# Expert stage: gate logits on four column tiles, and the second expert bias added on VectorE

## Chip, cores and metric

One core of one Trainium2 chip runs the whole program. The metric is the device time of one execution in microseconds; less is better. The number to compare with is the median of the runs.

## What is computed

Two layers on x of shape (4, 256, 256). The first is a cross attention with small heads. The second is a transformer block: layer norm, attention with 16 heads of 128, and a mixture of four experts on the 1024 tokens. The change touches only the experts:

```python
def _moe(h, w_gate, we1, be1, we2, be2):          # E = 4, I = 256, TOP_K = 2
    x = h.reshape(-1, d)                          # 1024 tokens x 256
    raw = softmax(x @ w_gate)                     # gate logits: 1024 x 4
    top_vals, top_idx = top_k(raw, TOP_K)
    w = softmax(top_vals)
    comb = zeros((t, E)).at[rows, top_idx].add(w) # gates: two per token are not 0
    hmid = gelu(einsum('td,edi->tei', x, we1) + be1)
    eout = einsum('tei,eid->ted', hmid, we2) + be2
    return einsum('te,ted->td', comb, eout)
```

`be2` is the second bias, one row of 256 per expert; it enters the output as gate times bias, summed over the experts. The block's result is multiplied by tanh of a scalar and added to x.

## The kernel before

The work is written out by hand, engine by engine, with semaphores between the engines; each engine runs its list in order. There is no scheduler. The tokens are eight tiles of 128 (`NT = 8`), in pairs of two tiles per batch entry (`B = 4`).

The experts come last. All four experts are computed for every token, and the gates weigh the results. TensorE splits each number into a high and a low part and makes three matmuls of each product (`three`, L1192). Its steps:

- `second_turn(b)`: four transposes that turn the normed rows of pair b; VectorE writes them, scaled, as `h2T` (L785, counted by `c_hT`), ScalarE makes the high part `hH`, GpSimd the low part `hL` (L446).
- `middle(n)`: n runs over 16; half the tokens (c = n // 8) by one half of an expert's inner columns, 6 matmuls of 512 columns into bank n % 2. It waits until ScalarE has read that bank (`c_gelu`, n - 1).
- ScalarE: `gelu` of the bank (L611) into `G`, and the high part into `GH` (L616); GpSimd subtracts for the low part `GL` (L450, counted by `c_gL`).
- `expert_out(m)`: m runs over 8 (half of the tokens times expert), 24 matmuls of 256 columns. It waits for `c_gL` 2m + 2, and from m = 2 on for VectorE's accumulation of m - 2 (`c_acc`).
- VectorE: for each m four instructions L1036 that add gate times result to `yacc`, and for the last expert of a half L1043, which finishes the output rows (`c_fin`) so that SyncE may store them.

The gates run beside this. TensorE makes the logits behind `expert_out(0)`: `h2T` is stationary (128 columns), the gate weights move (4 columns), eight tiles by two halves of the sum, in fp32, which is two instructions for one matmul (L1351). VectorE copies them (L981) and works out the gates in some 30 small instructions, with two exponentials on ScalarE between (L604, L606). ScalarE takes these in its own list ahead of `gelu(4)`; each change between exponential and gelu has a load of its function table. Then TensorE turns the gates (L1358, behind `middle(5)`), VectorE copies them to `V` as `combT` (L1017, L1018), TensorE multiplies them by `be2_sb`, four rows of stationary and moving data (L1366, behind `middle(6)`), and VectorE adds the four banks to `yacc` (L1023), before the first L1036.

TensorE's list there is: `second_turn(2)`, `middle(2)`, `second_turn(3)`, `middle(3)`, `expert_out(0)`, logits, `expert_out(1)`, `middle(4)`, `middle(5)`, turned gates, `middle(6)`, bias matmuls, `middle(7)`, `expert_out(2)`, and then `middle(8)`, `middle(9)`, `expert_out(3)` and so on, with `expert_out(6)` and `expert_out(7)` at the end with nothing between.

The cross attention at the start of the program has a step that uses four column tiles already, `x_values` (L1145): the stationary block has 32 columns, and four matmuls write partitions 0, 32, 64 and 96 of one bank.

```python
ins = pe.matmul(bank[4][32 * n:32 * (n + 1), t * P:(t + 1) * P], v_slots[:, XG * (2 * b + kt) + k // 3, :],
                probs[:, p % 4, n * P:(n + 1) * P], start=(z != 2), stop=(z != 1))
```

`stg` holds incoming attention weights; its last use is by GpSimd and ScalarE in the attention stage (`wqk_ready`, `wv_ready`). SyncE's list has 16 loads at the start, then 64 swaps, each as two DMAs of half a tile (L266 to L268), then the four stores of the output.

## Time and profile before

| | us |
|---|---|
| median of 3 runs | 505.7 |
| all runs | 510.95, 505.7, 505.22 |
| the profiled execution, device time | 508.26 |
| its span, first to last instruction | 506.4 |
| TensorE busy (3396 instructions) | 453.2 |
| VectorE busy (1163) | 367.1 |
| ScalarE busy (613) | 239.6 |
| GpSimd busy (318) | 232.8 |

The mean granted clock of TensorE over the span is 0.975 of full. The profile gives instructions by their line in the kernel; PE is TensorE's matmul, PEld its weight load, DVE VectorE, ACT ScalarE, POOL GpSimd, SP SyncE. A matmul's duration includes the time that it takes to run through the array, so the starts of successive ones say more than the durations. In the profile's rows the tile names have no digits, so `be2_sb` reads `be_sb` there.

### The profile page before, as it was taken

The numbers are of one execution on the slowest core, as the hardware profiler recorded it, in microseconds if no ns is written. First come the engines' busy times: TensorE is split into PE (matmuls) and PEld (weight loads), VectorE is DVE, ScalarE is ACT, GpSimd is POOL, SyncE is SP. The second block draws the span as 40 slices with busy tenths as digits, with TensorE's granted clock in tenths as the row PEclk, the third lists the DMA queues.
The fourth block names the chain that finished last, engine by engine and source line by source line (L and its number), as shares of the span: only waits on it lengthen the run. The fifth ranks groups of instructions, "written<-read, shape, count | busy, mean of one in ns | idle before, by whom it ended". The sixth has DMA issues, their size and how long they took to land.

```text
span 506.4 us, 10710 instructions
## 1 busy us (share of the span) xinstructions
PE 453.2 (89%) x3396; PEld 386.2 (76%) x3396; DVE 367.1 (72%) x1163; ACT 239.6 (47%) x613; POOL 232.8 (46%) x318
## 2 busy tenths in 40 slices
PE   0289998898777999999999999999999998689996
PEld 0166666675565899999999999999999997578895
DVE  5876669776557878788788887887877878835544
ACT  2026555453113555555655546556455565164342
POOL 5945709710345545446446445346454431162342
PEclk9999999999979999999999999999999998897899
DMA  8100000200123343352342532532533310000011
GB/s 286 28 3 1 2 1 3 84 1 1 23 62 84 72 119 84 84 145 64 78 133 58 143 85 62 145 74 52 144 83 83 77 29 0 2 0 2 0 43 42
DMA packets 19881, 31.41 MB, mean 62 GB/s; under 512 B 6020, under 2 KB 8200, under 8 KB 19848
## 3 DMA queue, kind: packets, MB, share of 16 engines
q1 hardware_dynamic: 15928, 22.31, 18.1%
q10 hardware_dynamic: 3920, 8.69, 5.7%
q8 instruction: 18, 0.29, 0.2%
q14 instruction: 15, 0.12, 0.1%
HBM read 13.16 MB, written 1.05 MB: 28 GB/s over the span
## 4 chain that ended last, share of the span: by engine, by line
PE 80%; DVE 12%; POOL 3%; issue 3%; DMA 1%; ACT 1%; ACTq 0%; DVEq 0%
PE bank L1192 42%; PE bank L1272 5%; PE bank L1235 5%; PE bank L1263 4%; PE bank L1145 3%; PE bank L1112 3%; PE bank L1273 3%; PE bank L1234 3%; PE bank L1126 2%; PE bank L1130 2%; PE bank L1090 1%; PE bank L1113 1%; PE bank L1128 1%; PE bank L1069 1%; DMA rows_sb<-in_rows 1%
## 5 line engine op out<-in xcount | busy, mean ns | idle before, releaser
L401 POOL TENSOR_TENSOR room<-room,qk_room 128x512 f32<-128x512 f32 x64 | 82.3, 1287 | 102.8 <-DMA qk_room<-qk_room 102.6
L542 ACT ACTIVATE probs<-sm,nm 128x128 f32<-128x128 f32 (+1 forms) x128 | 57.3, 448 | 116.2 <-DVE nm L917 116.2
L1192 PE MATMUL bank<-hH,qk_parts 128*128 128x512 f32 x256 | 81.0, 398 | 0.0
L840 DVE SCALAR_TENSOR_TENSOR qk_room<-bank,qk_bias,cst_sb 128x512 f32<-128x512 f32 x64 | 48.0, 750 | 37.2 <-PE bank L1192 35.8
L1192 PE MATMUL bank<-hL,qk_parts 128*128 128x512 f32 x128 | 62.4, 488 | 6.6 <-DVE room L840 5.7
L1192 PEld LDWEIGHTS bank<-hH,qk_parts 128*128 128x128 f32 x256 | 48.8, 191 | 10.1
L840 DVE SCALAR_TENSOR_TENSOR room<-bank,qk_bias,cst_sb 128x512 f32<-128x512 f32 x64 | 47.6, 743 | 0.0
L1192 PE MATMUL bank<-woH,o_parts 128*128 128x256 f32 x256 | 47.2, 283 | 0.0
L810 DVE TENSOR_REDUCE nxm<-bank 128x2 bf16<-128x512 f32 (+1 forms) x48 | 32.5, 688 | 14.9 <-PE bank L1113 14.3
L500 ACT ACTIVATE probs<-bank 128x512 f32<-128x512 f32 x48 | 28.6, 596 | 26.1 <-PE bank L1130 25.4
L1192 PE MATMUL bank<-woL,o_parts 128*128 128x256 f32 x128 | 39.0, 305 | 1.1 <-DVE o_parts L905 1.1
L1192 PEld LDWEIGHTS bank<-woH,o_parts 128*128 128x128 f32 x256 | 40.0, 192 | 0.0
L1272 PE MATMUL bank<-probs,V 128*128 128x256 f32 x128 | 39.0, 387 | 0.6 <-DVE o_parts L905 0.6
L1192 PE MATMUL bank<-wvL,hH 128*128 128x256 f32 x128 | 39.3, 307 | 0.0
L1235 PE MATMUL bank<-room 128*128 128x256 f32 x128 | 38.2, 380 | 0.0
L1192 PE MATMUL bank<-wvH,hH 128*128 128x256 f32 x128 | 36.4, 284 | 0.0
L450 POOL TENSOR_TENSOR qk_parts<-G,o_parts 128x512 fp32r<-128x512 f32 x16 | 20.7, 1298 | 34.0 <-ACT o_parts L616 33.5
L1192 PE MATMUL bank<-wvH,hL 128*128 128x256 f32 x128 | 36.3, 283 | 0.0
L1263 PE MATMUL bank<-cst_sb,probs 128*128 128x128 f32 x192 | 31.7, 274 | 4.9 <-DVE probs L961 4.9
L351 POOL TENSOR_TENSOR qk_parts<-stg,qk_parts 128x256 fp32r<-128x256 f32 x32 | 23.8, 743 | 26.5 <-ACT qk_parts L566 26.5
L556 ACT ACTIVATE o_parts<-bank,bv_pair 128x256 fp32r<-128x256 f32 x64 | 30.3, 474 | 11.6 <-PE bank L1273 10.8
L1263 PEld LDWEIGHTS bank<-cst_sb,probs 128*128 128x128 f32 x192 | 24.4, 140 | 14.6 <-DVE probs L961 6.8
(200 smaller groups left out, 1242.2 us busy)
## 6 DMA issues: line engine op xcount, KB each, us to landing
qk_room<-qk_room SPq DMA_DIRECT2D x128, 128.0 KB, 2.3
stg<-in_wqkv ACTq DMA_DIRECT2D x6, 768.0 KB, 4.6
stge<-in_we ACTq DMA_DIRECT2D x7, 256.0 KB, 3.2
stg<-in_wqkv SPq DMA_DIRECT2D x2, 768.0 KB, 6.4
stgo<-in_wo ACTq DMA_DIRECT2D x6, 256.0 KB, 3.6
x_sb<-in_x SPq DMA_DIRECT2D x4, 256.0 KB, 6.2
out_y<-yacc SPq DMA_DIRECT2D x4, 256.0 KB, 2.3
cst_sb<-in_cst SPq DMA_DIRECT2D x1, 520.0 KB, 6.9
```

Source lines behind the costliest of these rows:

```text
L351: pool.tensor_tensor(wqkL[:, c], stg[:, k, :, r * HD:(r + 1) * HD], wqkH[:, c].bitcast(F32), ALU.subtract).then_inc(s["wqk_ready"], 1)
L401: pool.tensor_tensor(v, v, qk_sw[:, q, :], ALU.subtract).then_inc(s["rope_done"], 1)
L450: pool.tensor_tensor(GL[:, (n // 2) % 2, n % 2, :], G[:, n % 2, :], GH[:, (n // 2) % 2, n % 2, :].bitcast(F32), ALU.subtract).then_inc(s[" ...
L500: act.activation(probs[:, p % 4, :], PT_B[p % 2][:, :], ACT.Exp).then_inc(s["s_exp"], 1)
L542: ins = act.activation(PR[:, q, a:e], sm[:, q, a:e], ACT.Exp, bias=nm[:, q, t:t + 1], scale=-1.0, accum_out=rs[:, q, t:t + 1])
L556: act.activation(oH[:, ((j - 2) // 2) % 2, q, :], bank[3][:, 0:256], ACT.Identity, bias=head_bias(j)).then_inc(s["b_oH"], 1)
L810: dve.tensor_reduce(nxm[:, m % 3, a:a + len(heads)], S_B[p % 2][:, :].rearrange("p (h n) -> p h n", h=len(heads)), AX.X, ALU.max, negate=T ...
L840: return dve.scalar_tensor_tensor(out.rearrange("p (b t) -> p b t", b=2), O_B[q][:, :].rearrange("p (b t) -> p b t", b=2), qk_bias[:, c:c ...
L1192: ins = pe.matmul(outp, l, r, start=(m == 0), stop=(m == n - 1))
L1235: pe.matmul(S_B[j % 2][:, P:3 * P], QT[:, 2 * r, second], QT[:, 2 * r + 1, both], start=True, stop=True).then_inc(s["b_s"], 1)
L1263: ins = pe.transpose(bank[2][:, n * P:(n + 1) * P], PR[:, 1 - q, n * P:(n + 1) * P], ident)
L1272: pe.matmul(bank[3][:, 0:256], V[:, 2 * b, r * HD:(r + 1) * HD], PTs[:, q, 0:256], start=True, stop=False)
```

## The change

The logits are made the other way round and earlier. The gate weights are stationary, padded with zeros from 4 to 32 columns (GpSimd clears `w_gate_sb` as its first instruction, and SyncE's load of it waits for that). For each half of the sum, four matmuls of 256 moving columns of `h2T`, one for each pair of tiles, write partitions 32b to 32b + 31 of bank 5. They stand in front of `expert_out(0)`. VectorE copies the 128x256 result to `nh`, TensorE turns it with two transposes in front of `expert_out(1)`, and VectorE copies four of each 32 columns as the logits. The gates are worked out as before.

The gates are no longer turned, and the bias is no longer a matmul. SyncE loads `be2`, repeated on all 128 partitions, into the space of `stg`, after the last swap. For each m VectorE adds gate times bias row to its four tiles of `yacc` (four new instructions, all operands in SBUF), before it waits for TensorE's result of that m.

```diff
-        w_gate_sb = sb("w_gate_sb", [P, KT, E])
-        be2_sb = sb("be2_sb", [E, D])
+        w_gate_sb = sb("w_gate_sb", [P, KT, 32])
...
+        be2_rows = stg[:, 0:2, :, :].rearrange("p w k n -> p (w k n)").rearrange("p (e n) -> p e n", e=E)
...
# SyncE
-            sp.dma_start(w_gate_sb[:, :, :], w_gate).then_inc(s["d_small"], 16)
-            sp.dma_start(be2_sb[:, :], be2).then_inc(s["d_small"], 16)
+            sp.wait_ge(s["gate_zero"], 1)
+            sp.dma_start(w_gate_sb[:, :, 0:E], w_gate).then_inc(s["d_small"], 16)
...
             steps(sp, step)
+            sp.wait_ge(s["wqk_ready"], 4 * NP)
+            sp.wait_ge(s["wv_ready"], NP)
+            sp.dma_start(be2_rows, be2.rearrange("(o e) n -> o e n", o=1).to_broadcast([P, E, D])).then_inc(s["d_be"], 16)
...
# GpSimd
+            pool.memset(w_gate_sb[:, :, :], 0.0).then_inc(s["gate_zero"], 1)
             link(pool.memset(room[:, 0:NT * XG * VP], 0.0))
...
# VectorE
             dve.wait_ge(s["c_logit"], 1)
-            link(dve.tensor_copy(Gt(0, 32), bank[5][:, 0:32]))
+            dve.tensor_copy(nh[:, 0, :], bank[5][:, 0:256]).then_inc(s["c_lgT"], 1)
+            dve.wait_ge(s["c_lg_pe"], 1)
+            link(dve.tensor_copy(Gt(0, 32).rearrange("p (b t e) -> p t b e", t=2, e=E),
+                                 bank[4][:, 0:256].rearrange("p (t b w) -> p t b w", t=2, b=B)[:, :, :, 0:E]))
...
-            dve.tensor_tensor(Gt(0, 32), Gt(120, 32), Gt(152, 32), ALU.add).then_inc(s["c_comb"], 1)
-            dve.wait_ge(s["c_combT_pe"], 1)
-            dve.tensor_copy(combT[:, 0:4, :].rearrange("p t n -> p (t n)"), bank[4][0:E, :])
-            dve.tensor_copy(combT[:, 4:8, :].rearrange("p t n -> p (t n)"), bank[5][0:E, :]).then_inc(s["c_combT"], 1)
-            for b in range(B):
-
-                dve.wait_ge(s["c_be"], b + 1)
-                y = yacc[:, 2 * b:2 * b + 2, :].rearrange("p t n -> p (t n)")
-                dve.tensor_tensor(y, y, bank[4 + b % 2][:, :], ALU.add).then_inc(s["c_init"], 1)
-            dve.wait_ge(s["c_init"], B)
+            link(dve.tensor_tensor(Gt(0, 32), Gt(120, 32), Gt(152, 32), ALU.add))
+            dve.wait_ge(s["d_be"], 16)
+            dve.wait_ge(s["b_yadd"], NU // 2)
 
             for m in range(2 * E):
 
                 c, e = divmod(m, E)
                 for hf in range(2):
                     b = 2 * c + hf
-                    dve.wait_ge(s["c_exp_pe"], 2 * m + hf + 1)
                     if m:
                         dve.wait_ge(s["c_acc"], 2 * (m - 1) + hf + 1)
+                    for t in range(2):
+                        n = 2 * b + t
+                        ins = dve.scalar_tensor_tensor(yacc[:, n, :], be2_rows[:, e, :], gate[:, 4 * n + e:4 * n + e + 1], yacc[:, n, :],
+                                                       ALU.mult, ALU.add)
+                    ins.then_inc(s["c_be"], 1)
+                for hf in range(2):
+                    b = 2 * c + hf
+                    dve.wait_ge(s["c_exp_pe"], 2 * m + hf + 1)
+                    dve.wait_ge(s["c_be"], 2 * m + hf + 1)
...
# TensorE
             middle(3)
+            pe.wait_ge(s["c_hT"], B)
+            pe.wait_ge(s["d_small"], 16)
+            pe.wait_ge(s["b_yadd"], NU // 2)
+            for k in range(KT):
+                for b in range(B):
+                    ins = pe.matmul(bank[5][32 * b:32 * (b + 1), 0:256], w_gate_sb[:, k, :], h2T[:, k, 256 * b:256 * (b + 1)],
+                                    start=(k == 0), stop=(k == 1))
+            ins.then_inc(s["c_logit"], 1)
             expert_out(0)
-            pe.wait_ge(s["c_hT"], B)
-            pe.wait_ge(s["d_small"], 32)
-            for n in range(NT):
-                for k in range(KT):
-                    ins = pe.matmul(bank[5][:, E * n:E * (n + 1)], h2T[:, k, n * P:(n + 1) * P], w_gate_sb[:, k, :], start=(k == 0), stop=(k == 1))
-            ins.then_inc(s["c_logit"], 1)
+            pe.wait_ge(s["c_lgT"], 1)
+            for t in range(2):
+                ins = pe.transpose(bank[4][:, t * P:(t + 1) * P], nh[:, 0, t * P:(t + 1) * P], ident)
+            ins.then_inc(s["c_lg_pe"], 1)
             expert_out(1)
             middle(4)
             middle(5)
-            pe.wait_ge(s["c_comb"], 1)
-            for n in range(NT):
-                ins = pe.transpose(bank[4 + n // 4][0:E, (n % 4) * P:(n % 4 + 1) * P], gate[:, E * n:E * (n + 1)], ident)
-            ins.then_inc(s["c_combT_pe"], 1)
             middle(6)
-            pe.wait_ge(s["c_combT"], 1)
-            for b in range(B):
-                if b >= 2:
-                    pe.wait_ge(s["c_init"], b - 1)
-                for t in range(2):
-                    ins = pe.matmul(bank[4 + b % 2][:, 256 * t:256 * (t + 1)], combT[:, 2 * b + t, :], be2_sb[:, :], start=True, stop=True)
-                ins.then_inc(s["c_be"], 1)
```

TensorE's list between the end of `middle(3)` and the first matmul of `expert_out(0)`, in the kernel before; a row names line, operation, output and inputs, and the semaphores waited for:

```order
L1192 MATMUL bank<-hL,weH 128x512
L1192 MATMUL bank<-hH,weL 128x512
L1192 MATMUL bank<-hH,weH 128x512
L1192 MATMUL bank<-weL,o_parts 128x256 [waits b_yadd,c_gL]
L1192 MATMUL bank<-weH,qk_parts 128x256
L1192 MATMUL bank<-weH,o_parts 128x256
```

The same place in the changed kernel, where the helper of the matmuls is at L1199 and the logits at L1358:

```order
L1199 MATMUL bank<-hL,weH 128x512
L1199 MATMUL bank<-hH,weL 128x512
L1199 MATMUL bank<-hH,weH 128x512
L1358 MATMUL bank<-qk_room,w_gate_sb 32x256 [waits b_yadd,d_small,c_hT]
L1358 MATMUL bank<-qk_room,w_gate_sb 32x256 x7
L1199 MATMUL bank<-weL,o_parts 128x256 [waits b_yadd,c_gL]
```

Eight logit matmuls have moved in front of `expert_out(0)`; before, sixteen of 128x4 stood behind it.

VectorE's list from the last instruction of the gates to the first accumulation, before:

```order
L1015 TENSOR_TENSOR gate<-gate 128x32 [waits dve_seq]
L1017 COPY V<-bank 4x512 [waits c_combT_pe]
L1018 COPY V<-bank 4x512
L1023 TENSOR_TENSOR yacc<-yacc,bank 128x512 [waits c_be] x4
L1036 SCALAR_TENSOR_TENSOR yacc<-bank,gate,yacc 128x256 [waits c_exp_pe,c_init]
L1036 SCALAR_TENSOR_TENSOR yacc<-bank,gate,yacc 128x256
```

And in the changed kernel, with the bias at L1034 and the accumulation at L1043:

```order
L1021 TENSOR_TENSOR gate<-gate 128x32 [waits dve_seq]
L1034 SCALAR_TENSOR_TENSOR yacc<-stg,gate,yacc 128x256 [waits b_yadd,d_be,dve_seq]
L1034 SCALAR_TENSOR_TENSOR yacc<-stg,gate,yacc 128x256 x3
L1043 SCALAR_TENSOR_TENSOR yacc<-bank,gate,yacc 128x256 [waits c_be,c_exp_pe]
L1043 SCALAR_TENSOR_TENSOR yacc<-bank,gate,yacc 128x256
```

The wait for turned gates and the four additions of banks are gone, and four bias instructions stand in front of the four accumulations, here and for each later m.

## Rows read from the trace of the kernel before

**Rows 1.** Stretches of the expert stage: busy time and count per engine, granted clock, DMA.
```profile
454.40:456.20 1.80, 1.80 (x11) 1.80 (x10) 0.00 (x0) 0.00 (x0) 0.00 (x0) 0.50 0.00 0
456.20:461.05 4.85, 4.85 (x24) 4.85 (x25) 3.94 (x24) 0.23 (x1) 0.00 (x0) 0.50 0.02 3
...
471.30:474.70 3.40, 3.40 (x15) 2.90 (x15) 3.09 (x8) 1.32 (x2) 0.78 (x1) 0.50 0.00 0
```

**Rows 2.** Timeline of TensorE: start, duration, line, tiles, shape, count.
```profile
448.95 0.28 PE L1192 MATMUL bank<-weL,o_parts 128*128 128x256 f32 x1
...
451.78 4.56 PE L1351 MATMUL bank<-w_gate_sb,qk_room 128*128 128x4 f32 x32
456.20 0.56 PE L1192 MATMUL bank<-weL,o_parts 128*128 128x256 f32 x1
...
461.30 0.40 PE L1192 MATMUL bank<-hL,weH 128*128 128x512 f32 x1
```

**Rows 3.** Timeline of TensorE, further on, to the start of `middle(8)`.
```profile
464.10 1.04 PE L1358 MATMUL bank<-cst_sb,gate 128*4 128x128 f32 x8
...
466.50 3.90 PE L1366 MATMUL bank<-be_sb,V 4*128 4x256 f32 x16
470.33 0.50 PE L1192 MATMUL bank<-hL,weH 128*128 128x512 f32 x1
...
476.24 0.40 PE L1192 MATMUL bank<-hL,weH 128*128 128x512 f32 x1
```

**Rows 4.** Timeline of TensorE in the cross attention: four column tiles.
```profile
61.77 0.43 PE L1145 MATMUL bank<-probs,room 128*32 128x128 f32 x8
62.13 0.28 PE L1112 MATMUL bank<-yacc,qk_room 128*128 128x256 bf16 x1
```

**Rows 5.** Timeline of VectorE; in brackets the idle time before and its releaser.
```profile
456.38 0.19 DVE L981 COPY gate<-bank 128x32 f32<-128x32 f32 x1 [7.63 <-PE bank L1351]
...
462.28 0.19 DVE L1015 TENSOR_TENSOR gate<-gate 128x32 f32<-128x32 f32 x1
...
471.16 3.23 DVE L1036 SCALAR_TENSOR_TENSOR yacc<-bank,gate,yacc 128x256 f32<-128x256 f32 x8
```

**Rows 6.** Timeline of ScalarE around `gelu(4)`.
```profile
461.29 1.28 ACT L611 ACT_TABLE_LOAD   x1
462.90 0.69 ACT L611 ACTIVATE G<-bank,cols_sb 128x512 f32<-128x512 f32 x1 [0.33 <-PE bank L1192]
```

**Rows 7.** Timeline of GpSimd: the low halves, early and late.
```profile
464.33 2.67 POOL L450 TENSOR_TENSOR qk_parts<-G,o_parts 128x512 fp32r<-128x512 f32 x2 [11.16 <-ACT o_parts L616]
...
496.13 2.69 POOL L450 TENSOR_TENSOR qk_parts<-G,o_parts 128x512 fp32r<-128x512 f32 x2 [2.93 <-ACT o_parts L616]
```

**Rows 8.** Timeline of VectorE at the end: last pair of m = 6, first of m = 7.
```profile
498.93 0.88 DVE L1036 SCALAR_TENSOR_TENSOR yacc<-bank,gate,yacc 128x256 f32<-128x256 f32 x2 [0.53 <-PE bank L1192]
500.61 0.88 DVE L1036 SCALAR_TENSOR_TENSOR yacc<-bank,gate,yacc 128x256 f32<-128x256 f32 x2 [0.81 <-PE bank L1192]
```

**Rows 9.** Timeline of TensorE: two waits before the expert stage.
```profile
426.67 0.69 PE L1263 MATMUL bank<-cst_sb,probs 128*128 128x128 f32 x3 [1.53 <-DVE probs L961]
...
445.20 0.66 PE L1296 MATMUL bank<-cst_sb,nh 128*128 128x128 f32 x4 [1.78 <-DVE nh L892]
```

**Rows 10.** Stretches of one us behind those waits.
```profile
427.00:428.00 1.00, 1.00 (x5) 0.78 (x3) 0.93 (x6) 0.49 (x1) 0.00 (x0) 0.50 0.00 0
...
445.00:446.00 1.00, 0.80 (x6) 0.75 (x7) 0.89 (x4) 1.00 (x2) 0.48 (x1) 1.00 0.00 0
```

**Rows 11.** DMA issues: KB each, median us from issue to landing.
```profile
stg<-in_wqkv ACTq DMA_DIRECT2D x6, 768.0 KB, 4.6
```

**Rows 12.** VectorE beside GpSimd: timeline, and L1043's durations in ns, min/median/max.
```profile
434.74 1.26 POOL L446 TENSOR_TENSOR hL<-qk_room,hH 128x512 fp32r<-128x512 f32 x1 [9.27 <-ACT hH L593]
435.08 0.94 DVE L643 SCALAR_TENSOR_TENSOR small<-small 128x2 f32<-128x2 f32 x1
...
L1043 DVE SCALAR_TENSOR_TENSOR yacc<-yacc,small,x_sb x4: 752/752/937, 481.6 to 503.1; 128x512 f32<-128x512 f32 x4
```

More of the change, by code:

```diff
@@ L118, in build_kernel @@
         gate = sb("gate", [P, 512])
-        combT = V[0:E, 0:4, :].rearrange("p t n -> p (t n)").rearrange("p (t n) -> p t n", t=NT)
+        be2_rows = stg[:, 0:2, :, :].rearrange("p w k n -> p (w k n)").rearrange("p (e n) -> p e n", e=E)
         qn = sb("qn", [P, 2, D])
@@ L164, in build_kernel @@
         b_s b_max b_exp b_norm b_pt b_ptcopy b_pv b_oH b_oL b_wo b_yadd v_pe v_ready
-        c_nh c_tr c_hT c_hH c_h c_logit c_comb c_combT_pe c_combT c_be c_init c_mid c_gelu c_gH c_gL c_exp_pe c_acc c_fin"""
+        c_nh c_tr c_hT c_hH c_h gate_zero d_be c_logit c_lgT c_lg_pe c_be c_mid c_gelu c_gH c_gL c_exp_pe c_acc c_fin"""
         s = {n: sem(n) for n in names.split()}
```

## The prediction

> **What bounds the kernel now.** The page comes first: it shows TensorE as the busiest engine, most of the chain that ended last on it, and its granted clock below full in a few slices near the end. All that the change touches on the compute engines lies from 448.95 us on, so the next view is a table of stretches from there. TensorE is busy without a break in all eight up to 500 us, and in three of them, 454.4 to 461.05 and 471.3 to 474.7, the granted clock is 0.50 [rows 1], that is 1.2 of 2.4 GHz. The timeline of TensorE says what stood there. The gate logits (L1351, 32 instructions of 4 columns) hold it from 451.78 to 456.20, 4.42 us, and `expert_out(1)` behind them takes 461.30 - 456.20 = 5.10 us [rows 2], while `expert_out(0)`, the same 24 matmuls, takes 451.78 - 448.95 = 2.83. The turned gates (L1358) and the bias matmuls (L1366, 466.50 to 470.33) are followed by `middle(7)` and `expert_out(2)` in 476.24 - 470.33 = 5.91 us [rows 3]; at full clock these are 1.40 (half of 464.10 - 461.30) and 2.83. So this part is TensorE bound, and thin matmuls cost twice there: their own time, and the fallen clock behind them. The clock fell while TensorE was busy; what went before it was L1351, and the second time L1366.
>
> **What is removed.** L1351 4.42. Slow `expert_out(1)` 5.10 - 2.83 = 2.27. L1358 with the small gap ahead of L1366: 466.50 - 464.10 less `middle(6)`'s 1.40, 1.00. L1366 3.83. Slow clock behind it 5.91 - 4.23 = 1.68. Together 13.2 us of the chain.
>
> **What TensorE gets.** Eight logit matmuls of 32 stationary and 256 moving columns, in fp32 two instructions each, so 16. The nearest row has the same layout with 128 columns: eight instructions on four column tiles take 62.13 - 61.77 = 0.36 us [rows 4]. Twice the instructions and twice the columns give 1.44 at most if the tiles go on running side by side. One after another, 16 fp32 instructions of 256 columns are L1366's: 3.83 us [rows 3]. If four do run at once the lower end is a quarter, 0.96. I take 1.15, between the near ends, and keep 3.8 for a rival. The wait for the last `h2T` costs nothing: VectorE was done with it at 456.38 - 7.63 = 448.75 [rows 5]. Two transposes: four took 0.66 us to their last result [rows 9]; for two I take 0.5 until VectorE starts (ends 0.35 and 0.66), and 0.2 of TensorE's issue. VectorE's new copy to `nh`, 256 columns out of PSUM like one instruction of L1036 (0.40, rows 5), lies beside `expert_out(0)`'s 2.83.
>
> **Where the gate chain then ends.** The logits end at 448.95 + 1.15 = 450.1, `expert_out(0)` at 452.93, and VectorE starts on the gates at 453.43 where it was 456.38 [rows 5]: 2.95 us earlier. From there the chain runs unchanged on VectorE and ScalarE, so the table load behind the second exponential moves from 461.29 to 458.34 and ends at 459.62 [rows 6]; `gelu(4)` starts at 459.65. TensorE gets there earlier: transposes until 453.15, `expert_out(1)` until 455.98, `middle(4)` and `middle(5)` until 458.78. `middle(6)` needs the bank that `gelu(4)` reads in 0.69 us [rows 6], so it starts at 460.4: **a new wait of 1.6 us**. `middle(6)` and `middle(7)` end at 463.2. `expert_out(2)` needs GpSimd's low halves of `gelu(4)` and `gelu(5)`; that pair ended at 464.33 + 2.67 = 467.00, 4.10 after `gelu(4)`'s start at 462.90 [rows 6, 7], so now at 463.75: a second wait of 0.6 us. `expert_out(2)` ends at 463.8 + 2.83 = 466.65, where it was 476.24 [rows 3]: 9.6 us. The other way round, 13.2 less 1.15, 0.2, 1.6 and 0.6 gives 9.65. VectorE is ready in time: gates done at 462.28 + 0.19 - 2.95 = 459.5, then four bias and four accumulate instructions at 3.23/8 = 0.40 us each [rows 5], until 462.8, before 463.75.
>
> **The bias on VectorE.** It adds 32 instructions of 128x256, four per expert call. L1043, all in SBUF, takes 0.75 for twice the columns [rows 12], and L1036 0.40 with one operand in PSUM [rows 5]; I use 0.40, so 12.8 us in all (ends 0.35 and, held by GpSimd, the last rival's). Per call VectorE then has 8 x 0.40 = 3.2 us against TensorE's 5.6 (two `middle` and one `expert_out`), and the bias stands ahead of the wait for TensorE's result, in time where VectorE idles. The exception is the last call, for `expert_out(7)` follows `expert_out(6)` with no `middle` between. VectorE's last accumulate pair of call 6 starts at 498.93; four bias instructions follow, and six at 0.393 end at 501.29, where call 7 started at 500.61 [rows 8]. What is behind it is VectorE's own, so **0.7 us comes back at the end**.
>
> **The clock behind the new wait.** A wait of 1.53 us before 426.67 was followed by clock 0.50, one of 1.78 before 445.20 by 1.00 [rows 9, 10]. The new one of 1.6 is between them. If the clock falls there, it covers `middle(6)` to `expert_out(2)`; 3.4 us at half clock, as from 471.3, cost up to 1.7, of which some 0.6 hides in the wait for GpSimd: 1.1. Ends 0 and 1.7; as one row of two says so, I take half of 1.1, 0.5. In the Trainium skill, "TensorE: Matmul & The Clock Gate" (Part 1, "What's actually happening") has the slow level return from idleness, after a wholly idle period; by that the term would be 0 and the time 496.8. The trace disagrees twice, with a fall at 454.4 while TensorE was busy [rows 1, 2] and one after 1.53 us of idling; the measurement decides.
>
> **What costs nothing.** GpSimd's clearing of the gate weights stands at the start, ahead of its wait for the DMA of `rows_sb`, and is hidden by it. SyncE's wait for it comes before SyncE's twelfth DMA, when the clearing is long done. The 512 KB copy of the bias rows is issued after the last swap, near 410 us, and is needed at 459.5; 768 KB landed in 4.6 us [rows 11]. Without that cover it would cost about 3 us. The four additions L1023 and both copies to `V` leave VectorE beside TensorE's work and are not counted again.
>
> **Sum.** 9.6 - 0.7 - 0.5 = 8.4 us. The profiled execution took 508.26 us (span 506.4), so it would be 499.9; the median of the runs is 505.7, 2.6 below it, and I take the same 8.4 from it: **497.3 us**, 1.7% faster. About 2% (10.1 us) is what a measurement of this kernel can tell from no change, so this counts as the same.
>
> **Rivals.**
> *More than 10 us.* The clock stays up (0.5), the logits take 0.96 (0.2), and the unprofiled runs had one slow stretch more in this part (1.7), since its fall need not be the same in each run: 10.8, 494.9 us. For it: two stretches hang on thin matmuls; against: the median is 2.6 us shorter than the profiled execution, which may as well mean fewer slow stretches.
> *Tiles one after another.* 3.8 instead of 1.15, and the whole gate chain moves with it: 2.65, 500.0 us. Against it speaks the 0.36 of rows 4: eight of half the columns in turn would be near 0.96.
> *The slow clock is not won.* The wait at `middle(6)` grows or repeats and the clock falls as often as before: the gain lacks the 2.27 + 1.68 but the term of 0.5 goes with it, 4.9 us, 500.8. For it: 1.6 and 0.6 us waits close together. Against: behind 463.8 TensorE has no cause to wait.
> *Slower: VectorE held by GpSimd.* The bias instructions read two tensors from SBUF. A 128x2 instruction of this kind took 0.94 us beside a GpSimd subtraction of 1.26, and one L1043 of four 0.94 instead of 0.75 [rows 12]. Held by h each, VectorE needs 3.14 + 4h per call against 5.62: it is the bound from h = 0.62, all the gain is gone at 0.92, and at a whole GpSimd instruction (1.29) seven calls lose 18.8 us, 516.1. Against it: GpSimd works 2.69 of 5.62 us, and the bias falls in its gap (call 6 from 494.2 to 495.8; GpSimd ends at 493.2 and starts at 496.13) [rows 7]; one held instruction at 462.8 has 2.8 us of slack. "GPSIMD Engine Reference" (Specifications) in the Trainium skill names the same conflict, for VectorE instructions with two SBUF inputs, and the trace agrees with 0.94; it gives no price.
>
> **How the numbers follow.** Forecast 0.63, with a range of its own of 495.8 to 499.2 (the ends of logits, transposes and clock); over 10 us 0.13; tiles in turn 0.12; slow clock not won 0.09; VectorE held 0.03. The range holds the forecast's own, the two rivals near 500 and most of the fast one: 494.6 to 500.8. Faster by over 2% 0.17 (its rival and the forecast's edge), slower by over 2% 0.02, within 0.81.
>
> **What would show it.** Logits near 1.15 us behind `middle(3)`; gates on VectorE 2.9 us earlier; one wait of TensorE for ScalarE of about 1.6 us at `middle(6)` and one for GpSimd of about 0.6 at `expert_out(2)`; bias instructions of 0.4 to 0.5 us with none near 1; the last accumulates 0.7 late behind four of them; clock 1.00 from 449 to 460. I am wrong if the clock falls in the logits or right behind them, if the wait at `middle(6)` is over 2.5 us, or if VectorE is what TensorE waits for at any `expert_out`.

## The result, and the profile after

The changed kernel takes 500.04 us (median of 6 runs, 498.48 to 502.3) against 506.39 of the kernel before on the same chip (6 runs, 503.2 to 510.95). The ratio is 0.9878, with a 95% interval of 0.9849 to 0.9908: 6.35 us or 1.2% faster, less than the 2% that tells a kernel from no change. The forecast was 497.3, and the result lies within its range of 494.6 to 500.8, near the slow end. The gain itself was forecast at 8.4 us, and that lies outside the measured interval, which is 4.7 to 7.6 us: near three quarters of it came.

The profiled execution took 499.90 us (span 498.1), 8.4 less than the profiled one of before, which is exactly the predicted difference. That agreement is partly luck, as the experiments show, for the medians are 6.35 apart. Single executions scatter by 2 to 3 us either way, and much of it arises before the experts: `middle(3)` ended between 444.8 and 450.8 us in the fourteen traces of this study; why is not followed here. So below a **local stretch** is compared: from the start of the first TensorE instruction behind `middle(3)` to the end of the last VectorE instruction. It was 503.85 - 448.95 = 54.90 us before; the times ahead of it are left out.

First the page of the changed kernel: busy time by engine, and the chain that ended last, by engine and by line.

```profile
PE 441.2 (89%) x3342; PEld 375.2 (75%) x3358; DVE 382.8 (77%) x1190; ACT 239.6 (48%) x613; POOL 233.5 (47%) x319
...
PE 68%; DVE 24%; issue 4%; POOL 1%; DMA 1%; ACT 1%; SPq 0%; DVEq 0%; POOLq 0%
PE bank L1199 35%; PE bank L1279 5%; PE bank L1242 5%; PE bank L1270 4%; DVE yacc L1034 3%; PE bank L1241 3%; PE bank L1280 3%; PE bank L1152 2%; DVE yacc L1043 2%; PE bank L1119 2%; DVE nxm L813 2%; PE bank L1137 2%; PE bank L1097 1%; PE bank L1135 1%; DVE small L646 1%
```

TensorE lost 12 us of busy time and VectorE gained 16. New are the two yacc lines, 5% of the span: the chain that ended last runs through VectorE's bias (L1034) and accumulation (L1043), some 25 us of the end. That is the first sign of a new bound.

TensorE's timeline from `middle(3)`'s end to `middle(8)`'s start, which answers to [rows 2, 3]:

```profile
448.44 1.07 PE L1358 MATMUL bank<-qk_room,w_gate_sb 128*32 128x256 f32 x16
449.44 0.39 PE L1199 MATMUL bank<-weL,o_parts 128*128 128x256 f32 x1
...
452.37 0.38 PE L1364 MATMUL bank<-cst_sb,nh 128*128 128x128 f32 x2
452.51 0.37 PE L1199 MATMUL bank<-weL,o_parts 128*128 128x256 f32 x1
...
455.42 0.40 PE L1199 MATMUL bank<-hL,weH 128*128 128x512 f32 x1
...
459.73 0.50 PE L1199 MATMUL bank<-hL,weH 128*128 128x512 f32 x1 [1.35 <-ACT G L614]
...
463.04 0.39 PE L1199 MATMUL bank<-weL,o_parts 128*128 128x256 f32 x1 [0.25 <-POOL qk_parts L453]
...
465.98 0.40 PE L1199 MATMUL bank<-hL,weH 128*128 128x512 f32 x1
```

The logits take 449.44 - 448.44 = 1.00 us; `expert_out(1)` 455.42 - 452.51 = 2.91, where it was 5.10; and the two forecast waits are there. The bracket at 459.73 counts 1.35 us of idling, since the view lets a matmul last until it has run through the array. By starts it is 1.5: `middle(5)`'s last matmul started at 457.99 and one takes 0.23 of pace. From `middle(3)`'s end to `middle(8)` it is 465.98 - 448.44 = 17.54 us, against 27.29 before.

Stretches of time there, with the columns of [rows 1]: the granted clock, third from the end, is 1.00 in all.

```profile
450.00:454.00 4.00, 4.00 (x36) 4.00 (x35) 0.81 (x5) 1.94 (x3) 2.69 (x3) 1.00 0.00 0
454.00:458.00 4.00, 4.00 (x26) 3.49 (x24) 3.38 (x22) 0.52 (x2) 0.00 (x0) 1.00 0.00 0
458.00:462.00 4.00, 2.65 (x12) 1.87 (x11) 3.86 (x13) 3.67 (x6) 1.58 (x2) 1.00 0.01 4
462.00:466.00 4.00, 3.75 (x29) 3.26 (x28) 4.00 (x5) 2.38 (x4) 3.72 (x3) 1.00 0.01 2
```

The gate chain on VectorE, ScalarE and GpSimd, which answers to [rows 5 to 7]:

```profile
452.79 0.19 DVE L986 COPY gate<-bank 128x32 f32<-128x32 f32 x1 [2.79 <-PE bank L1364]
...
458.68 0.19 DVE L1021 TENSOR_TENSOR gate<-gate 128x32 f32<-128x32 f32 x1
```

```profile
450.44 1.28 ACT L607 ACT_TABLE_LOAD   x1
...
457.69 1.28 ACT L614 ACT_TABLE_LOAD   x1
458.99 0.69 ACT L614 ACTIVATE G<-bank,cols_sb 128x512 f32<-128x512 f32 x1
```

```profile
460.42 2.57 POOL L453 TENSOR_TENSOR qk_parts<-G,o_parts 128x512 fp32r<-128x512 f32 x2 [7.73 <-ACT o_parts L619]
463.27 2.99 POOL L453 TENSOR_TENSOR qk_parts<-G,o_parts 128x512 fp32r<-128x512 f32 x2 [0.28 <-ACT o_parts L619]
```

`middle(3)` ended 0.51 us earlier than in the trace of before. With that taken off, each link is within 0.25 us of where it was put: the gates begin at 452.79 (forecast 453.43), the table load ends at 458.97 (459.62), the pair of low halves at 462.99 (463.75).

VectorE from there to the end of the program. In the text, call m is `expert_out(m)` with what VectorE does for it, m from 0 to 7. L1034 is the bias, L1043 the accumulation, L1050 the last step of the rows of the output.

```profile
462.06 4.48 DVE L1034 SCALAR_TENSOR_TENSOR yacc<-stg,gate,yacc 128x256 f32<-128x256 f32 x4
466.46 1.65 DVE L1043 SCALAR_TENSOR_TENSOR yacc<-bank,gate,yacc 128x256 f32<-128x256 f32 x4
468.03 2.71 DVE L1034 SCALAR_TENSOR_TENSOR yacc<-stg,gate,yacc 128x256 f32<-128x256 f32 x4
...
474.71 1.76 DVE L1050 SCALAR_TENSOR_TENSOR yacc<-yacc,small,x_sb 128x512 f32<-128x512 f32 x1
...
485.55 3.74 DVE L1034 SCALAR_TENSOR_TENSOR yacc<-stg,gate,yacc 128x256 f32<-128x256 f32 x4
...
490.79 1.66 DVE L1034 SCALAR_TENSOR_TENSOR yacc<-stg,gate,yacc 128x256 f32<-128x256 f32 x4
492.37 0.86 DVE L1043 SCALAR_TENSOR_TENSOR yacc<-bank,gate,yacc 128x256 f32<-128x256 f32 x2
493.26 0.75 DVE L1050 SCALAR_TENSOR_TENSOR yacc<-yacc,small,x_sb 128x512 f32<-128x512 f32 x1
493.93 0.87 DVE L1043 SCALAR_TENSOR_TENSOR yacc<-bank,gate,yacc 128x256 f32<-128x256 f32 x2
494.84 0.75 DVE L1050 SCALAR_TENSOR_TENSOR yacc<-yacc,small,x_sb 128x512 f32<-128x512 f32 x1
```

And the two lines over the whole program, durations in ns (min/median/max):

```profile
L1034 DVE SCALAR_TENSOR_TENSOR yacc<-stg,gate,yacc x32: 470/475/1524, 458.9 to 492.0; 128x256 f32<-128x256 f32 x32
...
L1043 DVE SCALAR_TENSOR_TENSOR yacc<-bank,gate,yacc x32: 468/472/481, 460.5 to 494.3; 128x256 f32<-128x256 f32 x32
```

No row after 458.9 has a bracket: VectorE works without a break to the end. The same shape of instruction never takes over 481 ns in this trace with one operand in PSUM, and up to 1524 with all in SBUF; four of the latter take 1.66 us undisturbed and 4.48, 2.71, 2.80 or 3.74 when GpSimd subtracts beside them. The last of the four of call 1, and the GpSimd instruction beside it:

```profile
465.03 1.51 DVE L1034 SCALAR_TENSOR_TENSOR yacc<-stg,gate,yacc 128x256 f32<-128x256 f32 x1
464.78 1.48 POOL L453 TENSOR_TENSOR qk_parts<-G,o_parts 128x512 fp32r<-128x512 f32 x1
```

VectorE's ends at 466.54 and GpSimd's at 466.26. An instruction that takes so much longer beside GpSimd's than alone is called held below.

TensorE's last matmul ends at 491.77 and VectorE at 495.59, 3.82 us later. That **tail** was 503.85 - 501.98 = 1.87 before. The forecast allowed 0.7 more; it is 1.95.

### The profile page after: what moved, and what is told of

Its sections match the earlier page's. It is cut to its first block, busy times and chain, and to the rows that moved or that the text cites. A ratio compares the mean times of both kernels' runs of the same rounds, so it can differ in the third digit from the quotient of the medians.

```text
span 498.1 us, 10649 instructions
## 1 busy us (share of the span) xinstructions
PE 441.2 (89%) x3342; PEld 375.2 (75%) x3358; DVE 382.8 (77%) x1190; ACT 239.6 (48%) x613; POOL 233.5 (47%) x319
## 3 DMA queue, kind: packets, MB, share of 16 engines
HBM read 13.68 MB, written 1.05 MB: 30 GB/s over the span
## 4 chain that ended last, share of the span: by engine, by line
PE 68%; DVE 24%; issue 4%; POOL 1%; DMA 1%; ACT 1%; SPq 0%; DVEq 0%; POOLq 0%
PE bank L1199 35%; PE bank L1279 5%; PE bank L1242 5%; PE bank L1270 4%; DVE yacc L1034 3%; PE bank L1241 3%; PE bank L1280 3%; PE bank L1152 2%; DVE yacc L1043 2%; PE bank L1119 2%; DVE nxm L813 2%; PE bank L1137 2%; PE bank L1097 1%; PE bank L1135 1%; DVE small L646 1%
## 5 line engine op out<-in xcount | busy, mean ns | idle before, releaser
L1199 PE MATMUL bank<-hH,qk_parts 128*128 128x512 f32 x256 | 82.2, 403 | 0.0
L1199 PE MATMUL bank<-hL,qk_parts 128*128 128x512 f32 x128 | 63.1, 493 | 6.5 <-DVE room L843 5.7
L1199 PEld LDWEIGHTS bank<-hH,qk_parts 128*128 128x128 f32 x256 | 49.6, 194 | 10.2
L1199 PE MATMUL bank<-woH,o_parts 128*128 128x256 f32 x256 | 46.5, 280 | 0.0
L1199 PE MATMUL bank<-woL,o_parts 128*128 128x256 f32 x128 | 38.5, 301 | 1.1 <-DVE o_parts L908 1.1
L1199 PE MATMUL bank<-wvL,hH 128*128 128x256 f32 x128 | 39.3, 307 | 0.0
L1199 PEld LDWEIGHTS bank<-woH,o_parts 128*128 128x128 f32 x256 | 39.2, 189 | 0.0
L1199 PE MATMUL bank<-wvH,hH 128*128 128x256 f32 x128 | 36.6, 286 | 0.0
L1199 PE MATMUL bank<-wvH,hL 128*128 128x256 f32 x128 | 36.5, 285 | 0.0
L480 ACT ACTIVATE qk_room<-bank 128x1024 bf16<-128x1024 bf16 x16 | 16.4, 1025 | 37.2 <-PE bank L1076 37.2
```

The costliest lines, as they stand in the source:

```text
L480: act.activation(qT[:, X, t, :, :].rearrange("p h n -> p (h n)"), bank_bf[0][:, :], ACT.Copy).then_inc(s["m6_free"], 1)
L1199: ins = pe.matmul(outp, l, r, start=(m == 0), stop=(m == n - 1))
```

## The experiments

Of the twelve runs two are the kernel before, one the changed kernel, seven are variants between or beside the two, and two are attempts to mend it. The kernel before was run beside each group: beside c0, e3, e4 and e5 its median was 506.49 us (11 runs), beside e1, e2, e6 and e7 506.26 (24 runs), beside b1, b2, e8 and e9, which ran on another chip than these eight, 505.78 (11 runs). Medians are compared through these, by their ratio. "To `middle(8)`" is the first part of the local stretch, and the wait is the bracket at `middle(6)`.

| kernel | local stretch | to `middle(8)` | wait | tail | median | ratio to before, 95% |
|---|---|---|---|---|---|---|
| before, profiled first | 54.90 | 27.29 | none | 1.87 | 506.39 | |
| before again, b1 | 53.27 | 25.67 | none | 1.87 | 504.68, one run | |
| before again, b2 | 53.24 | 25.66 | none | 1.86 | 506.75, one run | |
| changed | 47.15 | 17.54 | 1.35 | 3.82 | 500.04 | 0.9849 to 0.9908 |
| changed again, c0 | 47.11 | 17.52 | 1.33 | 3.84 | 499.37 | 0.9814 to 0.9916 |
| e1, new logits, old bias | 50.41 | 22.82 | none | 1.86 | 503.29 | 0.9912 to 0.9975 |
| e2, old logits, new bias | 49.27 | 19.67 | 1.25 | 3.84 | 501.78 | 0.9900 to 0.9971 |
| e7, thin matmuls put back | 50.64 | 21.04 | none | 3.84 | 503.57 | 0.9917 to 0.9969 |
| e4, no second bias | 45.11 | 17.51 | 1.36 | 1.87 | 497.57 | 0.9791 to 0.9879 |
| e3, bias rows in PSUM | 47.12 | 18.84 | 2.67 | 2.55 | 498.99 | 0.9805 to 0.9886 |
| e6, last bias one call earlier | 47.12 | 17.52 | 1.34 | 3.83 | 499.69 | 0.9847 to 0.9926 |
| e5, both | 47.23 | 19.63 | 2.68 | 1.87 | 500.32 | 0.9821 to 0.9912 |
| e8, both, table load ahead | 45.09 | 17.51 | 1.35 | 1.86 | 496.15 | 0.9800 to 0.9866 |
| e9, e8 and earlier transposes | 44.46 | 16.86 | 0.70 | 1.87 | 495.88 | 0.9773 to 0.9848 |

**c0: the changed kernel again**, with no edit.

> The changed kernel once more, as the base for the runs beside it. Its two traces so far are one (after). Theory: gain on the kernel before near 8.4 us in the profiled execution and near 6.3 in the median; in the trace again some of the 32 bias instructions (L1034) take 1 to 1.5 us instead of 0.47, all of them while GpSimd works, and VectorE is busy without a break from the gates to the end. Rival (chance of one execution): the long ones don't come back, and the last TensorE instruction is followed by 2.6 us of VectorE (1.9 as before plus the 0.7 of the sum) and not by about 4.

The local stretch repeats to 0.04 us and so do the wait and the tail, while the profiled executions differ by 2.7 us (497.24 and 499.90). The held bias instructions come back as well: four take 4.47, 2.70, 2.79 and 3.73 us in the calls where the first trace has 4.48, 2.71, 2.80 and 3.74. So an effect of 0.5 us can be read from the local stretch, and not from a median of six, as long as the same clock falls lie in both stretches.

**e1: the new logits with the old bias.** The turned gates, bias matmuls and four additions are those of before; VectorE's bias instructions are gone.

```diff
 # TensorE, behind middle(5) and middle(6), on the changed kernel
+            pe.wait_ge(s["c_comb"], 1)
+            for n in range(NT):
+                ins = pe.transpose(bank[4 + n // 4][0:E, (n % 4) * P:(n % 4 + 1) * P], gate[:, E * n:E * (n + 1)], ident)
+            ins.then_inc(s["c_combT_pe"], 1)
             middle(6)
...
+                    ins = pe.matmul(bank[4 + b % 2][:, 256 * t:256 * (t + 1)], combT[:, 2 * b + t, :], be2_sb[:, :], start=True, stop=True)
```

> New logits (four column tiles, in front of expert_out(0)), old bias (gates turned, matmuls of four rows, additions of banks on VectorE). Theory (own times and fallen clock, by the sum): it wins L1351's 4.42 and the slow 2.27 less 1.0 for the new logits and 0.2 for the transposes, less the wait of 1.4 at middle(6), so 4.1 us on the kernel before; the clock still falls behind L1366. Rival 1 (the gates are ready earlier, so nothing waits and the clock behind L1366 stays up too): 5.7. Rival 2 (the clock is won only when both thin kinds go): 1.9.

**e2: the old logits with the new bias.** Thin logit matmuls behind `expert_out(0)`, no padding and no transposes; the bias as in the changed kernel.

```diff
 # TensorE, on the changed kernel; the eight column-tile matmuls and the two transposes are taken out
             expert_out(0)
+            for n in range(NT):
+                for k in range(KT):
+                    ins = pe.matmul(bank[5][:, E * n:E * (n + 1)], h2T[:, k, n * P:(n + 1) * P], w_gate_sb[:, k, :], start=(k == 0), stop=(k == 1))
```

> Old logits (32 instructions of 4 columns behind expert_out(0)), new bias on VectorE from SBUF. Theory: the 1.0 for turned gates, 3.83 for L1366 and 1.68 of fallen clock go, 6.5, less 2.0 that the end gives back and less a new wait of TensorE for gelu(4) at middle(6), none here since the slow expert_out(1) covers it: 4.5 us on the kernel before, and the clock still falls behind L1351. Rival: VectorE, whose gates come 3.6 us later than in the changed kernel while TensorE has the same work behind them, makes TensorE wait at expert_out(2) or (3) and gives back more than 3 us: 3 us or less on the kernel before.

Each half is faster than before by itself, by 0.6% (both intervals leave out 1). Locally, against the 53.25 us of b1 and b2 further down, e1 wins 2.8 and e2 4.0. Expected were 4.1 and 4.5: e1's sum took the 4.42 and 2.27 of the first trace, and e2's took its slow `expert_out(1)` as cover for the wait. e1 has the old tail of 1.86, e2 the new one of 3.84: the lost tail belongs to the bias, not to the logits. In e1 the clock still falls behind the bias matmuls: `middle(7)` and `expert_out(2)` take 469.73 - 463.62 = 6.11 us. There is no wait at `middle(6)` in e1, but TensorE waits 0.54 us for the gates that it is to turn. e2 held a surprise. Its 32 thin matmuls take 3.48 us, not 4.42, and behind them the clock stayed up. So `expert_out(1)` was not slow, and the wait at `middle(6)`, for which "none" was expected, was 1.25 us. These are the stretches of e2 at the end of the thin matmuls (until 453.29) and in `expert_out(1)`, columns as in [rows 1]:

```profile
452.00:453.00 1.00, 1.00 (x11) 1.00 (x11) 0.00 (x0) 0.00 (x0) 0.00 (x0) 1.00 0.00 0
...
454.00:455.00 1.00, 1.00 (x11) 1.00 (x10) 0.64 (x4) 0.23 (x1) 0.00 (x0) 1.00 0.00 0
```

**e7: the thin matmuls put back into the changed kernel.** They write an unused part of bank 5, read by nobody: extra work, to price them with all else as it is.

```diff
             expert_out(0)
+            for n in range(NT):
+                for k in range(KT):
+                    pe.matmul(bank[5][:, 256 + E * n:256 + E * (n + 1)], h2T[:, k, n * P:(n + 1) * P], w_gate_sb[:, k, 0:E], start=(k == 0), stop=(k == 1))
```

> The changed kernel with the old 32 thin logit instructions put back as extra work behind expert_out(0), with their results used by nobody. Theory (thin matmuls cost twice): expert_out(1) takes about 5.1 us instead of 2.9 at a granted clock of 0.50, and the gate chain starts 4.4 us later since its transposes stand behind them; the time is that of the changed kernel plus 4.4 for the chain, and with the fallen clock hidden in the wait at middle(6), so 504.5 at 500.0 for the changed kernel. Rival (the clock fell for another reason at that place): clock 1.00 behind them, expert_out(1) 2.9 us, and the same 4.4 us.

They take 3.49 us, at full clock, and here the fall follows them; stretches of e7:

```profile
453.00:457.00 4.00, 4.00 (x38) 4.00 (x38) 0.01 (x1) 0.00 (x0) 0.25 (x1) 1.00 0.01 4
457.00:459.00 2.00, 2.00 (x15) 2.00 (x14) 1.53 (x10) 0.23 (x1) 0.00 (x0) 0.70 0.00 0
459.00:461.00 2.00, 2.00 (x11) 2.00 (x11) 1.83 (x13) 0.00 (x0) 0.00 (x0) 0.50 0.00 0
```

`expert_out(1)` takes 461.09 - 456.71 = 4.38 us instead of 2.91. That is 3.5 + 1.5 = 5.0 us more work, and the stretch grows by 3.5, since the wait of 1.5 at `middle(6)` is gone: it was only there because TensorE came too early. That the fall hides in the wait came as expected; the 4.4 and 5.1 us, taken from the first trace, did not. The medians differ by 3.7 us, each taken against its own kernel before (6.35 and 2.69).

**b1 and b2: the kernel before, twice more**, with no edit, for their traces.

> The kernel before once more, for its trace. Asked: does TensorE's granted clock fall in every execution behind the fourth middle? Theory (the fall comes in some executions only): from the end of middle(3) to the end of the last VectorE instruction the profiled execution of before took 54.9 us, with the 32 gate matmuls at 4.42 us and the expert_out after them at some 5.1 us; in one of these two executions at least the gate matmuls take 3.5 us, the expert_out 2.9 us, and the stretch 50 to 52.6 us. Rival (the fall comes every time, and the difference between the profiled executions and the medians lies upstream of middle(3)): 54.9 us within 0.4 us both times.

> The same as the run before it, a second execution: theory, the stretch from the end of middle(3) to the end is anything from 50 to 55 us, by whether the clock fell; rival, 54.9 us within 0.4 us.

In b1 both theories miss: the fall comes, so the stretch is not as short as 50 to 52.6, and it is not 54.9 either. In b2 the width of "50 to 55" held, but the same fall stands in it. TensorE's timeline of b1, at the places of [rows 2]:

```profile
449.88 3.63 PE L1351 MATMUL bank<-w_gate_sb,qk_room 128*128 128x4 f32 x32
453.37 0.36 PE L1192 MATMUL bank<-weL,o_parts 128*128 128x256 f32 x1
...
457.81 0.39 PE L1192 MATMUL bank<-hL,weH 128*128 128x512 f32 x1
```

The thin matmuls take 3.49 us and the `expert_out` behind them 4.44, 7.93 together, and in b2 the same to 0.01. In the execution that the prediction was read from they took 4.42 + 5.10 = 9.52. The stretches of b1 show why:

```profile
453.00:454.00 1.00, 1.00 (x10) 1.00 (x10) 0.39 (x3) 0.00 (x0) 0.00 (x0) 1.00 0.00 0
454.00:455.00 1.00, 1.00 (x7) 1.00 (x6) 0.64 (x4) 0.23 (x1) 0.00 (x0) 0.55 0.00 0
...
457.00:458.00 1.00, 1.00 (x7) 1.00 (x7) 0.88 (x7) 0.00 (x0) 0.00 (x0) 0.75 0.00 0
```

The clock is down from about 454.1 to 457.5, some 3.4 us, and in b2 likewise; in the first profiled execution it was down from 454.3 to 461.05, twice as long [rows 1]. The second fall, behind the bias matmuls, is the same in all three: `middle(7)` and `expert_out(2)` take 5.91, 5.88 and 5.87 us. So the part that differs is worth 9.52 - 7.93 = 1.59 us, and the local stretch of 53.25 less the changed kernel's 47.15 is 6.1 us, beside 6.35 between the medians. The 7.75 us between the first two traces (54.90 - 47.15) is more than the medians' 6.35 by about this one long fall.

**e4: the second bias left out.** VectorE's 32 bias instructions are taken away and nothing takes their place, so the output lacks the second bias.

```diff
-                        ins = dve.scalar_tensor_tensor(yacc[:, n, :], be2_rows[:, e, :], gate[:, 4 * n + e:4 * n + e + 1], yacc[:, n, :],
-                                                       ALU.mult, ALU.add)
-                    ins.then_inc(s["c_be"], 1)
```

> The 32 bias instructions left out, so the second bias is missing from the output; all else as in the changed kernel. Theory: 2.0 us less than the changed kernel, the same as e5, since in e5 the bias lies wholly in VectorE's idle time. Rival (VectorE's bias also delays TensorE early, at expert_out(2) or (3)): over 2.5 us less.

The tail is 1.87 again and the stretch 2.0 us shorter, with the way to `middle(8)` unchanged at 17.51. All that the bias costs is in the tail.

**e3: the bias rows in PSUM.** After the first exponential ScalarE copies the rows into banks 4 and 5, free by then, and VectorE reads them from there. Everything is computed.

```diff
 # ScalarE, around the first exponential of the gates
+                    act.wait_ge(s["d_be"], 16)
...
+                    for h in range(2):
+                        act.activation(bank[4 + h][:, :], be2_rows[:, 2 * h:2 * h + 2, :].rearrange("p e n -> p (e n)"), ACT.Copy).then_inc(s["be_psum"], 1)
 # VectorE
-                        ins = dve.scalar_tensor_tensor(yacc[:, n, :], be2_rows[:, e, :], gate[:, 4 * n + e:4 * n + e + 1], yacc[:, n, :],
+                        ins = dve.scalar_tensor_tensor(yacc[:, n, :], bank[4 + e // 2][:, 256 * (e % 2):256 * (e % 2 + 1)], gate[:, 4 * n + e:4 * n + e + 1], yacc[:, n, :],
```

> Same 32 bias instructions, but ScalarE copies the bias rows to two free banks of PSUM (two instructions of 512 columns between the two exponentials, where it idles 3.77 us), so each bias instruction has one operand in SBUF and one in PSUM. Theory (GpSimd holds the instructions with two SBUF inputs): no bias instruction over 0.5 us, VectorE idles again in front of TensorE's results, and the end is 1.3 us earlier than in the changed kernel (the 2.0 that the end lost, less 0.7 that the number of instructions costs). Rival (the number of instructions fills VectorE, 64 at 0.40 and the finishing ones): the time stays within 0.4 us of the changed kernel.

**e6: the last call's bias one call earlier.** The four bias instructions of call 7 stand ahead of the accumulations of call 6; rows stay in SBUF.

```diff
-            for m in range(2 * E):
+            def bias(m, needed):
...
+            for m in range(2 * E):
...
+                if m < 2 * E - 1:
+                    bias(m, ("c_acc", 2 * (m - 1) + 1) if m else None)
+                if m == 2 * E - 2:
+                    bias(m + 1, ("c_be", 2 * m + 1))
```

> The changed kernel with its bias rows in SBUF, and the four bias instructions of the last call in front of the accumulations of the call before. Theory (VectorE is behind at the end because GpSimd held it): moving four instructions wins nothing where VectorE has no idle time, so within 0.3 us of the changed kernel. Rival (only the four instructions at the end cost): 0.7 us less.

**e5: both edits together.**

> As e3, and the four bias instructions of the last call stand in front of the accumulations of the call before it, where VectorE idles. Theory: 0.7 us less than e3 and 2.0 less than the changed kernel, from the last TensorE matmul to the end as in the kernel before (1.9 us of VectorE). Rival (the end hangs on TensorE's result and not on the four instructions): same as e3. It computes the whole of the reference and would be the fastest version.

The three settle what makes the tail. With the rows in PSUM (e3) no bias instruction is held: all 32 of them, in the line of the groups, as count | sum, mean ns | idle before:

```profile
L1037 DVE SCALAR_TENSOR_TENSOR yacc<-bank,gate,yacc 128x256 f32<-128x256 f32 x32 | 13.2, 475 | 0.0
```

In the changed kernel the mean was 696 ns. VectorE then idles again between the calls, and the tail is 2.55, that is 0.68 over the old 1.87, which is the 0.7 of the forecast. Moving the last bias alone (e6) gives nothing, 3.83: where VectorE is busy without a break it does not matter where its work stands. Both together (e5) give the old 1.87. So of the tail's 1.95 us, 0.68 is the bias of the last call standing behind call 6, and 1.3 comes from the instructions that GpSimd holds; the first can only be won once the second is.

But e3 and e5 won nothing overall, because the wait at `middle(6)` grew from 1.35 to 2.67. ScalarE's timeline in e3 and TensorE's wait:

```profile
451.98 1.28 ACT L608 ACT_TABLE_LOAD   x1 [3.09 <-DVE gate L992]
```

```profile
459.53 0.50 PE L1202 MATMUL bank<-hL,weH 128*128 128x512 f32 x1 [2.67 <-ACT G L617]
```

The load of the exponential's table had stood at 450.44 in the changed kernel, idle time of ScalarE, well ahead of the input at 453.4. In e3 a second wait, for the bias rows, stands ahead of the exponential, and the load starts only when VectorE has made the input, though the rows had landed long before: 1.28 us come onto the gate chain. That would be an error of the edit and not of the idea, and e8 tests it. In e5 the clock also fell, near the end of the wait, and with the same wait in e3 it did not; e5:

```profile
463.00:465.00 2.00, 1.57 (x4) 1.29 (x5) 2.00 (x7) 1.94 (x4) 0.89 (x1) 0.50 0.06 12
```

**e8: e5 with the wait for the bias rows behind the exponential.**

```diff
-                    act.wait_ge(s["d_be"], 16)
                     act.wait_ge(s["c_gmax"], 1)
                     act.activation(gate[:, 64:96], gate[:, 32:64], ACT.Exp).then_inc(s["c_gexp"], 1)
+                    act.wait_ge(s["d_be"], 16)
                     for h in range(2):
```

> On the changed kernel: second bias rows in PSUM, copied by ScalarE after the first exponential (so that the table load is ahead of the gate chain again), and the last call's bias put on the sum one call earlier. Theory (VectorE is the bound at the end because its SBUF-only multiply-adds are held beside GpSimd's subtractions, and the earlier PSUM kernel lost its gain to a table load on the gate chain): the wait at middle(6) is back at 1.3 to 1.5 us from 2.7, the VectorE tail behind TensorE's last matmul is 1.9 us from 3.8, the stretch from the end of middle(3) to the end is 45.1 us (47.1 in the changed kernel), and the median is 1 to 2.5 us below the changed kernel's on this chip. Rival (the wait at middle(6) has another cause than the table load's place): the wait stays at 2.7 us, and the stretch at 47.1 us within 0.3.

The theory's numbers came: wait 1.35, tail 1.86, stretch 45.09, the 2.0 us of e4 with the whole result computed. The changed kernel has no runs on e8's chip. Through the kernel before, the ratios are 0.9833 and 0.9878, and their intervals overlap; that e8 is the faster is shown by the stretch. VectorE's timeline at the end of e8, four bias instructions of call 6 and four of call 7 in one piece and none held:

```profile
480.17 3.22 DVE L1036 SCALAR_TENSOR_TENSOR yacc<-bank,gate,yacc 128x256 f32<-128x256 f32 x8
483.59 0.88 DVE L1055 SCALAR_TENSOR_TENSOR yacc<-bank,gate,yacc 128x256 f32<-128x256 f32 x2 [0.20 <-PE bank L1211]
```

**e9: e8 with the two transposes of the logits between the halves of `expert_out(0)`.**

```diff
+                    if hf == 0 and between:
+                        between()
...
-            expert_out(0)
-            pe.wait_ge(s["c_lgT"], 1)
-            for t in range(2):
-                ins = pe.transpose(bank[4][:, t * P:(t + 1) * P], nh[:, 0, t * P:(t + 1) * P], ident)
-            ins.then_inc(s["c_lg_pe"], 1)
+            expert_out(0, turn_logits)
```

> The kernel before it in this call, with the two transposes of the logits put between the two halves of expert_out(0), 1.4 us earlier. Theory (middle(6) waits for the gelu that stands behind the gates' exponential and table load, so that gates that are 1.4 us earlier end that wait): the wait at middle(6) falls to 0 to 0.2 us, the one at expert_out(2) stays at some 0.5 us, and the stretch from the end of middle(3) is 43.7 to 44.2 us. Rival (the gelu or GpSimd behind it has another last input): the wait only moves to expert_out(2) or stays, and the stretch is within 0.3 us of the kernel without this edit.

The wait at `middle(6)` halves, to 0.70, and the stretch loses 0.63 us; neither the 0 to 0.2 nor the "nothing" of the rival. VectorE and GpSimd in e9 say what is between:

```profile
450.22 0.19 DVE L991 TENSOR_REDUCE gate<-gate 128x8 f32<-128x32 f32 x1
450.44 0.95 DVE L992 TENSOR_TENSOR gate<-gate 128x32 f32<-128x32 f32 x1
```

```profile
450.04 1.30 POOL L449 TENSOR_TENSOR hL<-qk_room,hH 128x512 fp32r<-128x512 f32 x1
```

L992 takes two SBUF inputs, and it takes 0.95 us where it takes 0.19 in e8: it ends only when GpSimd's last `hL` does (450.44 + 0.95 = 451.39, 450.04 + 1.30 = 451.34). Half of the earlier start is lost in that hold. The median, 495.88, can't be told from e8's 496.15; the local stretch can, by one trace of each.

## Why the prediction was right, and where not

- **What bounds the kernel, and the rows that go.** Right: TensorE until `middle(8)`. 27.29 - 17.54 = 9.75 us went there between the two profiled executions, against "9.6".
- **"What TensorE gets".** 1.15 was taken for the logits and they took 1.00, near the end of 0.96: four column tiles run side by side at 256 columns too. That rival ("tiles one after another") fell.
- **The gate chain and the waits.** "A new wait of 1.6 us" was 1.5, "a second wait of 0.6" about 0.4 (463.04 - 459.73 is 3.31, less twelve matmuls at 0.233 and 0.1 more for the first); the transposes and the start of the gates were right within 0.15. The chain of start times, carried over unchanged, was the sound part of the argument.
- **What is removed: mis-sized for a typical run.** The terms "L1351 4.42" and "5.10 - 2.83 = 2.27" come from one execution in which the clock was down for twice as long as in b1, b2 and e7. In b1 and b2 they are 3.49 and 1.61, together 1.59 less. This 1.59 and the 1.3 us missed at the end, less the 0.5 kept for a clock fall that did not come, put the measured gain 2 us below the forecast. The prediction saw that the fall "need not be the same in each run", but priced this only in the rival with more than 10 us gained. The other sign, "fewer slow stretches" in the typical run, it named as an argument against that rival and gave no term; b1 and b2 showed this sign. How often the long fall comes is open: it stands in one trace of three.
- **The clock behind the new wait, 0.5.** It did not fall in the changed kernel's two traces, nor in e2, e3, e4, e6, e8 and e9 (the granted clock is 1.00 behind the wait); once, in e5, with a wait of 2.68 us, it did. The term was 0 here.
- **"0.7 us comes back at the end".** The mechanism is right (e3: 0.68) and the sum too small: the tail grew by 1.95. The step that failed is in the last rival, "VectorE held by GpSimd": "the bias falls in its gap". It does so where VectorE idles: in e8 the bias of call 6 starts at 480.17, and GpSimd's pairs end at 479.27 and start at 482.20. But when the gates were done, at 458.9, the results of calls 0 and 1 had long been there, and VectorE worked on both without a gap. The bias of call 1, from 462.06, lay beside the pair that ends at 462.99 and the one that starts at 463.27, and took 4.48 us instead of 1.66. So VectorE fell behind by 2.8 us more, never idled again, and met GpSimd's pairs in later calls too: the bias is held in four of the eight (1, 2, 5 and 6), and once L1050. Whether it would have caught up without the holds of call 1 alone, no run tried. "One held instruction at 462.8 has 2.8 us of slack" was the sentence that failed: 2.82 us more in four instructions, at most 1.05 each, means three held ones, which used up the slack. TensorE waited for VectorE at no `expert_out`, so the price stayed at 1.3 us at the end and was not the 18.8 of that rival.
- **The sum.** 9.6 - 0.7 - 0.5 = 8.4 was forecast. For a typical run it is 8.1 (25.67 - 17.54) - 2.0 - 0 = 6.1. The 8.4 between the profiled executions is 9.75 - 2.0, 0.5 from ahead of the experts (448.95 - 448.44) and 0.1 from outside both spans; it met the forecast because the 1.3 missed at the end, the 0.5 not lost to the clock and these 0.6 nearly cancel. That is luck. "The slow clock is not won" would have ended near the measured median for another reason: the clock was won.

Of the signs it named, "bias instructions of 0.4 to 0.5 us with none near 1" and "the last accumulates 0.7 late" went against it; the others came.

## What to carry to other kernels

An instruction moved to an idle engine brings its operands' memory with it: VectorE at 3.2 us per 5.6 looked half idle, but with both tensors in SBUF and GpSimd subtracting from SBUF beside it, it was busy without a break for the last 37 us and set the end; a copy of one operand in a free PSUM bank took that away. That version, e8, takes 496.15 us, 9.6 below the kernel before on its chip, where the changed kernel was 6.4 and 7.1 below on its own. Its local stretch is 2.0 us shorter than the changed kernel's. Where a term of a sum is a fallen clock, take it from two or three traces, since one may hold a fall of double length. And a new wait belongs behind the first activation that needs another table, not ahead of it.
